# Two residual sums of a software-pipelined encoder chain: VectorE in place of GpSimd

## The chip, the core and the metric

The kernel runs on one core of a Trainium2 chip. The core has five engines with an instruction queue each: PE (TensorE) multiplies and transposes matrices into PSUM, DVE (VectorE), ACT (ScalarE) and POOL (GpSimd) work element by element, SP issues the transfers. Each engine goes through its own queue strictly in order and waits at semaphores for the others. The metric is the device time of one execution in microseconds (us).

## The reference

The input is `x`, four sequences of 1024 tokens with 128 features, all float32. The reference computes two parts after each other, each with a layer norm in front and a residual sum behind:

```python
x = x + encoder(layernorm(x))       # first part: 8 blocks, the one that the change touches
x = x + local_attention_stack(layernorm(x))   # second part: 6 layers of windowed attention and a gated FFN

# one block of the first part (linear attention)
q, k, v = x @ Wq + bq, x @ Wk + bk, x @ Wv + bv
Q, K = elu(q) + 1, elu(k) + 1
KV, Ksum = sum_n(K * v), sum_n(K)
V = Q * KV / (Q * Ksum + 1e-6)
x = layernorm(gelu(V @ Wo + bo) + x) * s1 + b1          # first residual sum
x = layernorm(gelu(gelu(x @ Wf1 + bf1) @ Wf2 + bf2) + x) * s2 + b2   # second residual sum
```

## The kernel before

Data stand with the 128 features on the partitions and tokens along the free dimension. The first part cuts the 4096 tokens into 8 chunks of 512 columns and runs 8 blocks over them: 64 chunk passes, numbered c = 0 to 63. All of it is written out as one software pipeline. Each engine has its own loop `for s in range(-7, CH)` with CH = 64, and in step s it works on chunks of different stages: queries of chunk s+7, keys, values and their exponentials of s+6, the attention's denominator and product of s+4, the first layer norm of s+3, the two FFN matmuls of s+2, the second sum and norm of s+1, and the end of chunk s. The order within a step is written by hand, apart for each engine, and nothing reorders it: the order in the text is the order in the queue.

What an engine does in a step, in its order:

- DVE: `denominator(s+4)` (L998), `invert(s+4, 1)` (L1004, a reciprocal over half a chunk), `query_min(s+6)` (L964), `norm_stats(s+3, 0)` (L1018 to L1026, the statistics of the first norm), `invert(s+4, 0)` (L1004), `key_min(s+6)` (L960), `query_round(s+6)` (L974), `query_up(s+6)` (L980), `attend(s+4)` (L1011), `norm_stats(s+1, 1)` (the same lines, second norm), `keys_up(s+6)` (L969), `key_values(s+6)` (L987, every second chunk with L991). With the first query of a block there is also `biases` (L955).
- POOL: `second_sum(s+1)` (L406), then `rstd_of` and `shift_of` of the first norm (L393, a power on 128x4; L398, a product on 128x4), the same two for the second norm, and `first_sum(s+4)` (L402).
- ACT: `hidden(s+2, 0)` (L786), `second_norm(s)` (L796), `hidden(s+2, 1)`, an activation table load, `query_exp(s+6)` (L763), `unit(s+3, 0)` (L773, scales with what L393 and L398 made), `key_exp(s+6)` (L759), `first_norm(s+3)` (L781), a table load, `hidden` 2 and 3 (L786), `attn_gelu(s+4)` (L767), `unit(s+1, 1)` (L773), `ff_gelu(s+2)` (L791).
- PE: `hidden(c, 0)` for c = s+2 (L551), `second_back(s)` and `first_turn(s+3)` (L492, four 128x128 transposes each), `hidden` 1, `down` 0 (L556), `key` (L497), `hidden` 3, `down` 1, `hidden` 2, `first_back(s+3)` and `second_turn(s+1)` (L492), `query` and `value` (L497), `project(s+4)` (L526), `down` 2 and 3.

The first sum adds the output of `attn_gelu`, g1, to the chunk's columns of X and writes z1, which `first_turn` transposes into PSUM for the statistics. The second sum adds the output of `ff_gelu`, g2, to x1 and writes z2 for `second_turn`. g1, g2, x1, z1 and z2 lie in SBUF with two buffers each. The semaphores `ga` (`attn_gelu`), `g2_r` (`ff_gelu`), `z1_r` and `z2_r` (`z1_ready`, `z2_ready`) carry these steps.

Of the kernel before, what the change touches and what calls it, by code (L numbers as in the profile page):

```python
# [14 lines left out]
ALU = mybir.AluOpType  # L15
# [53 lines left out]
def build(nc, xT, wa1, wa2, wb, wf, rot, mask, outT):  # L69
    with ExitStack() as ctx:  # L70
        def sb(name, shape):
            return ctx.enter_context(nc.sbuf_tensor(name, shape, F32))
# [10 lines left out]
        X = sb("X", [P, NB * SP1])  # L83
# [43 lines left out]
        mk, mq, K_, den, V_, g1, g2, x1, z1, z2, zn1, zn2 = (parts[2 * i:2 * i + 2] for i in range(12))  # L127
# [55 lines left out]
        def seq_col(b, t):  # L183

            return b * SP1 + 1 + t
# [11 lines left out]
        def live(n):  # L197

            return not isinstance(n, int) or 0 <= n < NT
# [14 lines left out]
        def on(c):  # L214

            return 0 <= c < CH

        def of(c):

            return c // NC, c % NC // UT, c % UT  # L220

        def x_at(c):

            _, b, u = of(c)
            return slice(seq_col(b, COL * u), seq_col(b, COL * u) + COL)
# [20 lines left out]
        def done(l, n, each=1):  # L246

            return each * (l * NT + n + 1) + 1
# [29 lines left out]
        def ln_rstd(pool, k, u, v):  # L278
            pool.wait_ge(LN[k]["stat"][u], 3 * v)
            pool.tensor_tensor(rstd[:, u, :], ve[:, u, :], power[:, 0:4], ALU.pow)\  # L280
                .then_inc(LN[k]["rstd"][u], 1)
# [90 lines left out]
        @block.gpsimd  # L372
        def _(pool):
            pool.memset(ident[:, :], 0.0).then_inc(consts, 1)
            pool.memset(power[:, :], -0.5).then_inc(consts, 1)
            pool.wait_ge(consts, 1)
            pool.affine_select(out=ident[:, :], in_=ident[:, :], compare_op=ALU.not_equal, fill=1.0, base=0,
                               pattern=[[-1, P]], channel_multiplier=1).then_inc(consts, 1)
            pool.memset(X[:, :], 0.0).then_inc(consts, 1)
            pool.memset(Y[:, :], 0.0).then_inc(consts, 1)  # L380
            pool.wait_ge(consts, 5)

            def pre_norm(k):
                with pool.Fori(0, NB) as b:
                    for u in U:
                        ln_rstd(pool, "pre", u, k * NB + b + 1)

            pre_norm(0)

            def rstd_of(c, i, stat, ready):  # L390
                k = 2 * i + c % 2
                pool.wait_ge(stat, 3 * c + 3)
                pool.tensor_tensor(rstdA[:, k, :], veA[:, k, :], power[:, 0:4], ALU.pow).then_inc(ready, 1)  # L393

            def shift_of(c, i, rstd_r, ready):
                k = 2 * i + c % 2
                pool.wait_ge(rstd_r, c + 1)
                pool.tensor_tensor(shiftA[:, k, :], mnegA[:, k, :], rstdA[:, k, :], ALU.mult).then_inc(ready, 1)  # L398

            def first_sum(c):  # L400
                pool.wait_ge(ga, c + 1)
                pool.tensor_tensor(z1[c % 2], g1[c % 2], X[:, x_at(c)], ALU.add).then_inc(z1_r, 1)  # L402

            def second_sum(c):
                pool.wait_ge(g2_r, c + 1)
                pool.tensor_tensor(z2[c % 2], g2[c % 2], x1[c % 2], ALU.add).then_inc(z2_r, 1)  # L406

            for s in range(-7, CH):
                if on(s + 1):
                    second_sum(s + 1)  # L410
                if on(s + 3):
                    rstd_of(s + 3, 0, st1_r, rs1_r)
                    shift_of(s + 3, 0, rs1_r, sh1_r)
                if on(s + 1):
                    rstd_of(s + 1, 1, st2_r, rs2_r)
                    shift_of(s + 1, 1, rs2_r, sh2_r)
                if on(s + 4):
                    first_sum(s + 4)
            pre_norm(1)


            for u in U:
                pool.wait_ge(x_done[u], NB * (BLOCKS + 2) + 1)
            pool.memset(PTd, 0.0).then_inc(consts, 1)
            pool.memset(kTf, 0.0).then_inc(consts, 1)
            pool.memset(vv[RING - 1], 0.0).then_inc(consts, 1)
            with pool.Fori(0, LAYERS) as l:
                def add_k(n):
                    pool.wait_ge(rotk_r, done(l, n))
                    pool.wait_ge(trk_mm, done(l, n - 1))  # L430
                    pool.tensor_tensor(tu[:, K], t1[:, K], t2[:, K], ALU.add).then_inc(addk_r, 1)  # L431

                def add_q(n):
                    pool.wait_ge(rotq_r, done(l, n))
                    pool.wait_ge(trq_mm, done(l, n - 1))
                    pool.tensor_tensor(tu[:, Q], t1[:, Q], t2[:, Q], ALU.add).then_inc(addq_r, 1)  # L436

                def probs_norm(n):
                    pool.wait_ge(rec_r, done(l, n))
                    pool.tensor_tensor(pe3, pe3, rr[:, :].unsqueeze(1).unsqueeze(3).to_broadcast([P, 2, HEADS, WIN]),  # L440
                                       ALU.mult).then_inc(p_r, 1)

                def unit_k(n):

                    pool.wait_ge(roots_r, done(l, n, ROOT_STEPS))
                    pool.wait_ge(addk_r, done(l, n))
                    pool.tensor_tensor(heads(tu[:, K]), heads(tu[:, K]), wide(rinv[:, HEADS:2 * HEADS], DH),  # L447
                                       ALU.mult).then_inc(k_r, 1)

                def unit_q(n):  # L450

                    pool.wait_ge(addq_r, done(l, n))
                    pool.tensor_tensor(heads(tu[:, Q]), heads(tu[:, Q]), wide(rinv[:, 0:HEADS], DH),  # L453
                                       ALU.mult).then_inc(q_r, 1)

                def step(n, r):
                    if live(n + 1):
                        add_k(n + 1)
                        add_q(n + 1)
                    if live(n - 1):  # L460
                        probs_norm(n - 1)
                    if live(n + 1):
                        unit_k(n + 1)
                        unit_q(n + 1)

                walk(pool, step)
                with pool.Fori(0, NB) as b:
                    for u in U:
                        ln_rstd(pool, "nf", u, l * NB + b + 1)
# [453 lines left out]
        def _(dve):  # L923
# [38 lines left out]
            def query_min(c):  # L962
                dve.wait_ge(qp_mm, c + 1)
                dve.tensor_scalar(mq[c % 2], ps[:, Q_BANK, :], bias(c, 1), 0.0, ALU.add, ALU.min).then_inc(mq_r, 1)  # L964
# [18 lines left out]
            def key_values(c):  # L983
                _, b, u = of(c)
                dve.wait_ge(vp_mm, c + 1)
                dve.wait_ge(K_r, c + 1)
                dve.scalar_tensor_tensor(K_[c % 2], ps[:, V_BANK, :], bias(c, 2), K_[c % 2], ALU.add, ALU.mult,  # L987
                                         accum_out=kvp[:, b % 2, u, 1:2]).then_inc(KV_r, 1)
                if u == UT - 1:
                    dve.wait_ge(KV_r, c + 1)  # L990
                    dve.tensor_tensor(kvs[:, b, :], kvp[:, b % 2, 0, :], kvp[:, b % 2, 1, :], ALU.add)\  # L991
                        .then_inc(ksum, 1)
# [21 lines left out]
            def norm_stats(c, i, turned, st):  # L1014
# [10 lines left out]
                dve.tensor_scalar(mnegA[:, k, :], mvA[:, k, :, 0], -1.0, None, ALU.mult)  # L1025
                dve.tensor_scalar(veA[:, k, :], mvA[:, k, :, 1], EPS_A, None, ALU.add).then_inc(st, 1)  # L1026

            for s in range(-7, CH):
                if on(s + 4):
                    denominator(s + 4)  # L1030
                    invert(s + 4, 1)
                if on(s + 6):
                    if (s + 6) % NC == 0:
                        biases(s + 6)
                    query_min(s + 6)
                if on(s + 3):
                    norm_stats(s + 3, 0, t1_mm, st1_r)
                if on(s + 4):
                    invert(s + 4, 0)
                if on(s + 6):  # L1040
                    key_min(s + 6)
                    query_round(s + 6)
                    query_up(s + 6)
                if on(s + 4):
                    attend(s + 4)
                if on(s + 1):
                    norm_stats(s + 1, 1, t2_mm, st2_r)
                if on(s + 6):
                    keys_up(s + 6)
                    key_values(s + 6)  # L1050
            for u in U:
                dve.wait_ge(x_done[u], NB * (BLOCKS + 1) + 1)
            pre_norm(1)
# [2 lines left out]
            with dve.Fori(0, LAYERS) as l:  # L1056
# [3 lines left out]
                for i in range(4):  # L1060
                    s = WB[:, B_SC + i * DH:B_SC + (i + 1) * DH].unsqueeze(1).to_broadcast([P, TS, DH])
# [215 lines left out]
```

## Time and profile before

| | before |
|---|---|
| median of 3 runs | 4459.96 us (4459.77 to 4462.57) |
| the profiled execution | 4460.07 us, its span 4458.3 us |
| first part's pipeline | from about 45 us to about 880 us of the span |
| busy over the whole span: PE, DVE, ACT, POOL | 86%, 79%, 76%, 53% |

The span is what the instructions cover; the execution's time is 1.8 us longer. The whole-span shares mix two parts with different limits. The change stands in the first part alone, so only rows of that part's steady stretch, with its fill and its drain, say what an edit there is worth. In the rows below, a busy instruction's start and duration are in us; "idle before" in brackets names the releaser of a wait. Two instructions that follow each other on DVE or ACT overlap by 0.05 to 0.1 us in the records, so the distance between two starts is what an instruction takes of its queue, and durations are a little longer.

### The profile page before, as it was taken

The page shows a single profiled execution, that of the slowest core. Times are in us where ns is not written, and L with a number is a line of the kernel's source. Part 1 is how long each engine was busy: PE and PEld are TensorE (multiplying, and loading weights), DVE is VectorE, ACT ScalarE, POOL GpSimd, SP SyncE. Part 2 cuts the span into 40 slices and gives each one's busy share as a digit, 9 for nine tenths or more (in the row PEclk, how much of TensorE's full clock was granted, in tenths as well). Part 3 has the DMA queues.
Part 4 walks back from the last instruction along what each step waited for, and adds up shares of the span by engine and source line. Part 5 has one row for each costly group of instructions (what it writes and reads, how often), then busy time and mean ns, then how long its engine had stood idle before and what let it go on. Part 6 is the DMA issues. An engine that isn't in the chain of part 4 may idle for free.

```text
span 4458.3 us, 132631 instructions
## 1 busy us (share of the span) xinstructions
PE 3846.2 (86%) x49248; PEld 2440.5 (55%) x49248; DVE 3501.2 (79%) x7236; ACT 3407.2 (76%) x9277; POOL 2377.6 (53%) x1420
## 2 busy tenths in 40 slices
PE   5999999869997699977899877999679997789977
PEld 2444444446664366653566634666436665366653
DVE  6999999679994689954899747999369995589964
ACT  3999999759995489963899836999349995389973
POOL 2444444357772377741777605777137773277750
PEclk8999999989998899988999989999889998899998
DMA  1000000013332033330333302333113332033330
GB/s 45 8 8 10 8 8 26 1 43 81 85 84 55 23 78 83 84 80 7 72 84 82 81 23 56 84 85 81 43 34 81 85 84 65 13 77 84 83 71 19
DMA packets 146282, 245.44 MB, mean 55 GB/s; under 512 B 43664, under 2 KB 69264, under 8 KB 144912
## 3 DMA queue, kind: packets, MB, share of 16 engines
q1 hardware_dynamic: 146064, 242.61, 22.9%
q8 instruction: 127, 2.08, 0.2%
q14 instruction: 91, 0.75, 0.1%
HBM read 26.43 MB, written 2.10 MB: 6 GB/s over the span
## 4 chain that ended last, share of the span: by engine, by line
PE 42%; ACT 27%; SPq 10%; issue 8%; DVE 7%; DMA 3%; POOL 2%; DVEq 0%; ACTq 0%; POOLq 0%
ACT arena L856 12%; PE ps L607 7%; PE ps L722 6%; ACT arena L872 5%; PE ps L556 5%; PE ps L551 5%; ACT arena L831 4%; PE ps L676 4%; PE ps L497 4%; SPq L336 3%; PE ps L731 3%; SPq L346 3%; PE ps L492 3%; DMA arena<-arena 3%; ACT arena L843 2%
## 5 line engine op out<-in xcount | busy, mean ns | idle before, releaser
L607 PE MATMUL ps<-WB,arena 128*128 128x512 f32 x2304 | 1102.3, 615 | 95.0 <-ACT arena L872 37.8
L856 ACT ACTIVATE arena<-arena,nmx 128x64 f32<-128x64 f32 x3072 | 1022.7, 337 | 12.1 <-DVE arena L1145 11.7
L607 PEld LDWEIGHTS ps<-WB,arena 128*128 128x128 f32 x2304 | 418.9, 195 | 510.8 <-issue 451.8
L431 POOL TENSOR_TENSOR arena<-arena 128x1024 f32<-128x1024 f32 x192 | 455.4, 2372 | 400.1 <-DVE arena L1075 397.9
L440 POOL TENSOR_TENSOR arena<-arena,rr 128x1024 f32<-128x1024 f32 x192 | 367.6, 1915 | 466.7 <-DVE rr L1139 466.7
L1068 DVE TENSOR_TENSOR arena<-ps,tables 128x1024 f32<-128x1024 f32 x384 | 468.5, 1220 | 168.9 <-ACT arena L831 168.5
L856 ACT ACTIVATION_READ_ACCUMULATOR arena<-arena,nmx 128x1 f32 x3072 | 585.6, 191 | 0.0
L676 PE MATMUL ps<-arena 128*64 128x64 f32 x12288 | 431.5, 232 | 132.8 <-DMA arena<-arena 108.4
L831 ACT ACTIVATE arena<-ps 128x1024 f32<-128x1024 f32 x384 | 388.5, 1015 | 177.1 <-PE ps L607 142.4
L676 PEld LDWEIGHTS ps<-arena 128*64 128x64 f32 x12288 | 408.6, 146 | 159.6 <-issue 157.4
L1075 DVE TENSOR_TENSOR arena<-ps,tables 128x512 f32<-128x512 f32 x768 | 491.1, 681 | 0.0
L637 PE MATMUL ps<-ident,arena 128*128 128x128 f32 x3072 | 413.9, 279 | 77.3 <-POOL arena L447 40.1
L637 PEld LDWEIGHTS ps<-ident,arena 128*128 128x128 f32 x3072 | 349.9, 143 | 210.6 <-POOL arena L447 99.5
L436 POOL TENSOR_TENSOR arena<-arena 128x1024 f32<-128x1024 f32 x192 | 455.1, 2370 | 7.0 <-PE ps L637 3.6
L1092 DVE TENSOR_REDUCE ssq<-arena 128x32 f32<-128x2048 f32 x192 | 437.0, 2276 | 0.0
L684 PE MATMUL ps<-arena,WB 128*128 128x128 f32 x3072 | 387.1, 281 | 20.1 <-ACT arena L864 20.1
L280 POOL TENSOR_TENSOR rstd<-ve,power 128x4 f32<-128x4 f32 x64 | 63.6, 1009 | 633.7 <-DVE ve L276 633.7
L872 ACT ACTIVATE arena<-ps 64x1024 f32<-64x1024 f32 x384 | 388.7, 1012 | 13.6 <-PE ps L607 11.4
L684 PEld LDWEIGHTS ps<-arena,WB 128*128 128x128 f32 x3072 | 368.4, 196 | 23.0 <-ACT arena L864 23.0
L447 POOL TENSOR_TENSOR arena<-arena,rinv 128x1024 f32<-128x1024 f32 x192 | 365.5, 1903 | 22.1 <-DVE rinv L1123 22.1
L661 PEld LDWEIGHTS ps<-arena 64*32 64x32 f32 x24576 | 267.5, 105 | 190.9 <-issue 185.8
L453 POOL TENSOR_TENSOR arena<-arena,rinv 128x1024 f32<-128x1024 f32 x192 | 365.7, 1905 | 0.0
(101 smaller groups left out, 6751.8 us busy)
## 6 DMA issues: line engine op xcount, KB each, us to landing
arena<-arena SPq DMA_DIRECT2D x768, 128.0 KB, 2.3
arena<-arena SPq DMA_DIRECT2D x1536, 64.0 KB
WB<-wb SPq DMA_DIRECT2D x6, 2176.0 KB, 8.6
arena<-X SPq DMA_DIRECT2D x384, 32.0 KB, 1.8
arena<-wa SPq DMA_DIRECT2D x8, 581.0 KB, 3.7
WF<-wf SPq DMA_DIRECT2D x6, 537.5 KB, 3.8
keep<-xT SPq DMA_DIRECT2D x1, 2048.0 KB, 7.7
outT<-keep SPq DMA_DIRECT2D x1, 2048.0 KB, 6.3
```

The lines of the kernel that those rows point to most:

```text
L431: pool.tensor_tensor(tu[:, K], t1[:, K], t2[:, K], ALU.add).then_inc(addk_r, 1)
L436: pool.tensor_tensor(tu[:, Q], t1[:, Q], t2[:, Q], ALU.add).then_inc(addq_r, 1)
L607: i = pe.matmul(banks[:, c, :], xs_[r], WB[:, w * INNER + c * COL:w * INNER + (c + 1) * COL], start=True, stop=True)
L637: i = pe.transpose(s_ps[:, j // 4, (j % 4) * P:(j % 4 + 1) * P], src[:, j * P:(j + 1) * P], ident[:, :])
L676: i = pe.matmul(o_ps[64 * a:64 * a + 64, side, c * 64:(c + 1) * 64], vv[r][:, side, h * DH:(h + 1) * DH], pw[:, side, :, a, c, :], start=T ...
L684: i = pe.matmul(o_ps[:, 0, 0:P], WB[:, B_WO + c * D:B_WO + (c + 1) * D], OT[:, c, :], start=(c == 0), stop=(c == NP - 1))
L831: act.activation(sq[:, half], src.rearrange("p b c -> p (b c)"), ACT.Square).then_inc(count, 1)
L856: i = act.activation(pe3[:, :, h, :], sc[:, 64 * h:64 * h + 64].rearrange("p (k q) -> p k q", k=2), ACT.Exp, bias=nmx[:, h:h + 1], accum_o ...
L872: i = act.activation(vv[r][rows, side, :], kv_ps[rows].rearrange("p b c -> p (b c)"), ACT.Copy)
L1068: dve.tensor_tensor(heads(t1[:, half]), src.rearrange("p b (h d) -> p (b h) d", d=DH), t, ALU.mult)
L1075: k = dve.tensor_tensor(heads(t2[:, half])[:, :, here], src.rearrange("p b (h d) -> p (b h) d", d=DH)[:, :, there], t, ALU.mult)
L1092: dve.tensor_reduce(ssq[:, :], heads(sq), AX_X, ALU.add).then_inc(red_r, 1)
```

## The change

The two functions `first_sum` and `second_sum` leave the POOL loop and stand in the DVE loop, with the same operands, the same waits and the same signals. `second_sum(s+1)` comes behind `query_min(s+6)` and ahead of `norm_stats(s+3, 0)`; `first_sum(s+4)` is the last thing of DVE's step. POOL keeps the powers and products on 128x4. No other engine's program changes.

```diff
@@ gpsimd
-            def first_sum(c):
-                pool.wait_ge(ga, c + 1)
-                pool.tensor_tensor(z1[c % 2], g1[c % 2], X[:, x_at(c)], ALU.add).then_inc(z1_r, 1)
-
-            def second_sum(c):
-                pool.wait_ge(g2_r, c + 1)
-                pool.tensor_tensor(z2[c % 2], g2[c % 2], x1[c % 2], ALU.add).then_inc(z2_r, 1)
-
             for s in range(-7, CH):
-                if on(s + 1):
-                    second_sum(s + 1)
                 if on(s + 3):
                     rstd_of(s + 3, 0, st1_r, rs1_r)
                     shift_of(s + 3, 0, rs1_r, sh1_r)
                 if on(s + 1):
                     rstd_of(s + 1, 1, st2_r, rs2_r)
                     shift_of(s + 1, 1, rs2_r, sh2_r)
-                if on(s + 4):
-                    first_sum(s + 4)
@@ vector
+            def first_sum(c):
+                dve.wait_ge(ga, c + 1)
+                dve.tensor_tensor(z1[c % 2], g1[c % 2], X[:, x_at(c)], ALU.add).then_inc(z1_r, 1)
+
+            def second_sum(c):
+                dve.wait_ge(g2_r, c + 1)
+                dve.tensor_tensor(z2[c % 2], g2[c % 2], x1[c % 2], ALU.add).then_inc(z2_r, 1)
+
             for s in range(-7, CH):
                 if on(s + 4):
                     denominator(s + 4)
...
                     query_min(s + 6)
+                if on(s + 1):
+                    second_sum(s + 1)
                 if on(s + 3):
                     norm_stats(s + 3, 0, t1_mm, st1_r)
...
                     key_values(s + 6)
+                if on(s + 4):
+                    first_sum(s + 4)
```

DVE's queue before, one step of the steady stretch from its last instruction on; the names in brackets are the semaphores that an instruction waits for:

```order
601 L987 SCALAR_TENSOR_TENSOR arena,kvp<-ps,arena 128x512 [waits K_ready,v_proj]
602 L991 TENSOR_TENSOR kvs<-kvp 128x2 [waits KV_ready]
603 L998 TENSOR_SCALAR arena<-arena,kvs 128x512 [waits seq_sums]
604 L1004 RECIPROCAL arena<-arena 128x256 [waits den_ready]
605 L964 TENSOR_SCALAR arena<-ps,arena 128x512 [waits q_proj]
606 L1018 BN_STATS statA<-ps 128x6 [waits z1_turned]
```

The same place of DVE's queue in the changed kernel (its lines are numbered 12 lower up to the two new functions):

```order
600 L975 SCALAR_TENSOR_TENSOR arena,kvp<-ps,arena 128x512 [waits K_ready,v_proj]
601 L979 TENSOR_TENSOR kvs<-kvp 128x2 [waits KV_ready]
602 L1018 TENSOR_TENSOR arena<-arena,X 128x512 [waits attn_gelu]
603 L986 TENSOR_SCALAR arena<-arena,kvs 128x512 [waits seq_sums]
604 L992 RECIPROCAL arena<-arena 128x256 [waits den_ready]
605 L952 TENSOR_SCALAR arena<-ps,arena 128x512 [waits q_proj]
606 L1022 TENSOR_TENSOR arena<-arena 128x512 [waits ff_gelu]
607 L1006 BN_STATS statA<-ps 128x6 [waits z1_turned]
```

The first sum (602) with its wait for `attn_gelu` now stands ahead of the denominator, the reciprocal and the query minimum, and the second sum (606) with its wait for `ff_gelu` ahead of the first norm's statistics. POOL's queue before, one step:

```order
103 L402 TENSOR_TENSOR arena<-arena,X 128x512 [waits attn_gelu]
104 L406 TENSOR_TENSOR arena<-arena 128x512 [waits ff_gelu]
105 L393 TENSOR_TENSOR rstdA<-veA,power 128x4 [waits n1_stats]
106 L398 TENSOR_TENSOR shiftA<-mnegA,rstdA 128x4 [waits n1_rstd]
107 L393 TENSOR_TENSOR rstdA<-veA,power 128x4 [waits n2_stats]
108 L398 TENSOR_TENSOR shiftA<-mnegA,rstdA 128x4 [waits n2_rstd]
```

Afterwards only the four instructions on 128x4 are left of it.

## Rows read from the trace of the kernel before

**Rows 1.** Busy time by engine in stretches of the first part (start:end, length, then engines)
```profile
core 0: us, PE busy (x) PEld busy (x) DVE busy (x) ACT busy (x) POOL busy (x), PEclk, DMA share, GB/s
100.00:820.00 720.00, 719.71 (x2353) 353.76 (x2352) 661.38 (x1912) 684.79 (x1175) 290.23 (x352) 1.00 0.03 11
...
844.00:856.00 12.00, 10.34 (x34) 4.84 (x34) 3.63 (x24) 8.80 (x19) 4.74 (x6) 1.00 0.01 1
```

**Rows 2.** Waits from 100 to 900 us (total us, times, longest): DVE, PE
```profile
DVE statA L1018 <- PE ps L492: 66.4, 97, 8.7
...
PE ps L492 <- POOL arena L406: 1.3, 1, 1.3
```

**Rows 3.** PE in order of time: back transposes of two steps in a row, and a late one
```profile
501.27 1.08 PE L492 MATMUL ps<-ident,arena 128*128 128x128 f32 x8
...
513.50 1.08 PE L492 MATMUL ps<-ident,arena 128*128 128x128 f32 x8
...
819.20 1.08 PE L492 MATMUL ps<-ident,arena 128*128 128x128 f32 x8
```

**Rows 4.** ACT in order of time, the same step
```profile
501.96 0.78 ACT L781 ACTIVATE arena<-ps,arena 128x512 f32<-128x512 f32 x1 [0.23 <-PE ps L492]
502.75 1.28 ACT L786 ACT_TABLE_LOAD   x1
504.05 1.27 ACT L786 ACTIVATE arena<-ps,arena 128x512 f32<-128x512 f32 x2
505.20 0.69 ACT L767 ACTIVATE arena<-ps,arena 128x512 f32<-128x512 f32 x1
...
507.15 0.73 ACT L791 ACTIVATE arena<-ps,arena 128x512 f32<-128x512 f32 x1
...
511.94 1.49 ACT L773 ACTIVATE arena<-ps,shiftA,rstdA 128x128 f32<-128x128 f32 x4
```

**Rows 5.** DVE in order of time, the same step
```profile
502.39 0.89 DVE L1018 BATCH_NORM_STATS2 statA<-ps 128x6 f32<-128x128 f32 x4 [0.49 <-PE ps L492]
...
505.73 0.49 DVE L998 TENSOR_SCALAR arena<-arena,kvs 128x512 f32<-128x512 f32 x1
506.25 1.75 DVE L1004 RECIPROCAL arena<-arena 128x256 f32<-128x256 f32 x1
507.92 0.65 DVE L964 TENSOR_SCALAR arena<-ps,arena 128x512 f32<-128x512 f32 x1
508.55 0.89 DVE L1018 BATCH_NORM_STATS2 statA<-ps 128x6 f32<-128x128 f32 x4
...
511.69 0.65 DVE L960 TENSOR_SCALAR arena<-ps,arena 128x512 f32<-128x512 f32 x1
512.26 0.42 DVE L974 TENSOR_SCALAR arena<-arena 128x512 f32<-128x512 f32 x1
...
513.38 0.74 DVE L1011 SCALAR_TENSOR_TENSOR arena<-arena,kvs 128x512 f32<-128x512 f32 x1
```

**Rows 6.** POOL in order of time, the same step and the next
```profile
505.97 1.38 POOL L402 TENSOR_TENSOR arena<-arena,X 128x512 f32<-128x512 f32 x1 [0.63 <-ACT arena L767]
507.95 1.28 POOL L406 TENSOR_TENSOR arena<-arena 128x512 f32<-128x512 f32 x1 [0.60 <-ACT arena L791]
...
518.21 1.10 POOL L402 TENSOR_TENSOR arena<-arena,X 128x512 f32<-128x512 f32 x1 [0.63 <-ACT arena L767]
```

**Rows 7.** All engines in the drain: a first norm's statistics and the scaling that waits for them
```profile
826.48 0.89 DVE L1018 BATCH_NORM_STATS2 statA<-ps 128x6 f32<-128x128 f32 x4 [0.54 <-PE ps L492]
...
829.47 1.51 ACT L773 ACTIVATE arena<-ps,shiftA,rstdA 128x128 f32<-128x128 f32 x4 [1.44 <-POOL shiftA L398]
```

**Rows 8.** A DVE sum of two SBUF operands; a DVE start released by ACT
```profile
879.95 1.30 DVE L935 TENSOR_TENSOR arena<-keep,X 128x512 f32 x2 [5.44 <-ACT X L796]
...
1409.75 0.69 ACT L917 ACTIVATE arena<-ps,WF 128x512 f32<-128x512 f32 x1
1410.58 0.75 DVE L1192 SCALAR_TENSOR_TENSOR arena<-ps,WF,arena 128x512 f32<-128x512 f32 x1 [5.12 <-ACT arena L917]
```

## The prediction, made before the changed kernel was run

> **What bounds the kernel now.** I read the first part alone: first the busy time by engine in its steady stretch, then the waits, then each engine in order of time over one step.
>
> The busy times [rows 1] show three engines close to full: from 100 to 820 us PE is busy for 719.71 of 720 us, ACT for 684.79, DVE for 661.38, and POOL, which carries the two sums, for 290.23. The granted clock there is 1.00, TensorE's upper level of 2.4 GHz.
>
> The length of a step comes from PE's back transposes (`first_back` and `second_turn`, L492) [rows 3]: they start at 501.27, at 513.50, and 26 steps later at 819.20, so a step takes (819.20 - 501.27) / 26 = 12.23 us. In 720 us there are 58.9 steps. DVE is thus busy for 661.38 / 58.9 = 11.23 us of a step and idle for 1.00 us, nearly all of it while it waits for transposes (66.4 us in 97 waits) [rows 2].
>
> What closes the step of 12.23 us is a loop between ACT and PE, not DVE and not POOL. I call the start of `first_back` F (501.27) and follow it. ACT's `first_norm` starts at F + 0.69, its table load at F + 1.48, `hidden` 2 and 3 at F + 2.78, `attn_gelu` at F + 3.93 and ends at F + 4.62 [rows 4]. From there ACT runs on, with two short waits for PE, to `unit(s+3)` at 511.94, and 1.56 us later PE starts the next `first_back` at 513.50 [rows 3, 4]. The statistics of DVE and the power of POOL come in time for that `unit`: the statistics start at 508.55 [rows 5]; in the drain, where ACT does wait for them, the distance from the statistics' start to `unit` is 829.47 - 826.48 = 2.99 us [rows 7]; so `unit` could start at 511.54 and starts at 511.94. That is a slack of 0.40 us. It is the number on which the forecast turns.
>
> The sums themselves are off this loop before the change. POOL's first sum starts 0.08 us behind `attn_gelu`, its second 0.07 us behind `ff_gelu` [rows 4, 6], and from 100 to 900 us PE waits once, for 1.3 us, for the second [rows 2].
>
> **What goes.** Two POOL instructions a step, 1.10 to 1.38 and 1.28 us [rows 6], 64 of each. Their readers, two groups of transposes, hardly ever wait for them, so I take a gain of 0. Its bounds are 0 and, if the 1.3 us of wait [rows 2] were all of it, about 1 us in the whole run. The exception is the very end, where nothing else is left to hide the last second sum: it gets some 0.5 us shorter, which I leave out.
>
> **What comes.** Two DVE sums of 128x512 float32 from SBUF. The trace of before has the same operation on DVE in L935, two in 1.30 us [rows 8], that is 0.61 us from start to start and 0.69 us for the last. The bounds for one in the queue are 0.57 us (a 128x512 form with one tensor operand, 511.69 to 512.26 [rows 5]) and 0.69 us. I take 0.61, since it is the same operation. DVE's own work becomes 11.23 + 1.22 = 12.45 us, already over the 12.23 us of a step.
>
> A rule speaks for the move: the Trainium skill, page "GPSIMD Engine Reference", section "4.1 Engine selection", sends elementwise sums to VectorE because GpSimd takes about twice as long. The trace agrees on the ratio (1.28 against 0.69 us, 1.9 times); what it would make of the time is the second rival below.
>
> **What moves, and where it gets on the path.** The changed order puts a wait for `attn_gelu` ahead of everything that DVE does in the next step. `attn_gelu` ends at F + 4.62 (505.89), and DVE before the change starts `denominator` already at 505.73, F + 4.46 [rows 4, 5]. So DVE now stands at the first sum until `attn_gelu` is through. Queued behind it are `denominator`, half of the reciprocals, `query_min`, the second sum and then the first norm's statistics, for which POOL, ACT and PE wait. The new chain, once round:
>
> - F to the end of `attn_gelu`: 4.62 us [rows 4].
> - ACT's end to DVE's start: 1410.58 - (1409.75 + 0.69) = 0.14 us [rows 8]; bounds 0.08 us (POOL's start behind ACT [rows 4, 6]) and some 0.2. I take 0.13.
> - first sum 0.61, `denominator` 0.52 (505.73 to 506.25), reciprocal 1.67 (to 507.92), `query_min` 0.57 (511.69 to 512.26, the same form without a wait behind it), second sum 0.61 [rows 5, 8]: 3.98 us.
> - statistics to `unit`: 2.99 us [rows 7].
> - `unit` to the next F: 1.56 us [rows 3, 4].
>
> The sum is 4.62 + 0.13 + 3.98 + 2.99 + 1.56 = 13.28 us against 12.23: **1.05 us more in each step**. The same seen from the slack: the statistics start 8.73 us behind F instead of 7.28 (508.55 - 501.27), 1.45 us later, of which 0.40 is slack.
>
> What else could be later is not. The second sum needs `ff_gelu`, which ends at F + 6.61 (507.15 + 0.73); DVE gets to it at F + 8.12. `first_turn` needs z1; the first sum ends at F + 5.4, and the transposes run one `second_back` behind `unit(s+1)`, after F + 6.2. The second norm's statistics start at F + 1.12 (502.39) for PE; DVE reaches them at F + 0.9, so they stay where they are, and DVE is ready for the first sum at F + 4.46 at the latest. DVE keeps about 0.2 us of wait there and 0.3 to 0.6 us in front of the first sum. PE gets about 1 us of idle time in front of each `first_back`. ACT waits before `unit`.
>
> **The clock.** The added holes in PE's work could cost granted clock. In the drain PE is busy for 10.34 of 12 us, with holes of that size, at a granted clock of 1.00 [rows 1]; the forecast has it busy for about 12.2 of 13.3 us. I take 0 for it; its bound above is in the last rival.
>
> **The sum.** The chain runs through the first sum and the next step's `query_min` in 61 steps (s = -4 to 56). 61 x 1.05 = 64 us. In the fill and at the last steps single terms differ by some tenths either way, which I leave out. The second part's instructions are the same. The profiled execution of before took 4460.07 us, 0.11 us from the median of the runs: 4460 + 64 = **4524 us**. With the bounds of the terms (each sum 0.57 to 0.69 twice, the start behind ACT 0.08 to 0.2) a step takes 13.15 to 13.51 us, and the time is 4516 to 4538 us.
>
> **The rivals.**
>
> 1. *DVE's own work is the bound, the chain isn't.* If DVE need not stand at `attn_gelu` (because ACT drifts ahead of it once DVE is slower), a step takes DVE's work alone: 12.45 us by its busy time, or 12.65 with the small gaps between its instructions, 0.22 to 0.42 us more, 61 steps: 4473 to 4486 us. For it: ACT has 12.23 - 684.79 / 58.9 = 0.60 us of idle time. Against it: `attn_gelu` hangs at a fixed distance behind F by ACT's own order, a table load and three activations, and F hangs on DVE's statistics. Chance 0.10.
> 2. *Faster: the slow sum was what PE waited for.* If POOL's second sum stood between `ff_gelu` and the transposes on the path, each step would win 1.28 - 0.69 = 0.59 us, 61 x 0.59 = 36 us: 4424 us. It decides where the second sum ends later than PE gets to `second_turn`. That it does not is in the rows: it ends at 509.23, and `second_turn` follows `first_back` of 513.50. The rule of the Trainium skill on elementwise sums ("GPSIMD Engine Reference", section 4.1) points this way. Chance 0.03.
> 3. *No change within what can be told* (0.2%, 9 us; about what a measurement of this kernel tells from no change). DVE's 1.00 us of idle takes the 1.22 us in, and the 0.40 us of slack the rest. It would need the wait for `attn_gelu` to cost nothing, at most 0.15 us a step. Chance 0.03.
> 4. *More than forecast.* Two prices. First, POOL and DVE hinder each other: POOL's first sum took 1.38 us where it started at 505.97, inside L998 (505.73 to 506.22), and 1.10 us in the next step [rows 5, 6]. If a DVE sum met a POOL power like that, 0.28 us a step would come in, 17 us: 4541 us. But the second norm's power and product are over some 3 us behind the statistics of F + 1.12, by F + 4.1, and the first sum starts at F + 4.75. Second, a lower clock at the holes: PE's own work of 12 us at half the clock in one step of ten would cost about 1.2 us a step, 73 us more, some 4597 us. Together 0.08.
>
> The Trainium skill, page "SBUF — State Buffer", section "SBUF: two separate sides", has a rule for the first of these: a DVE operation with two SBUF inputs and a GpSimd operation hold one port pair in turn, the loser waits for the whole instruction. The trace agrees in that L402's long case ends 1.13 us behind the end of L998, its own length. By that rule the move is safe only as long as the two do not meet, and would else cost up to 17 us by the sum above.
>
> **How the numbers follow.** The forecast has 0.76, the rivals 0.10, 0.03, 0.03 and 0.08. 8 in 10 are reached with the forecast's own bounds, 4516 to 4538, widened on both sides for the fill, for terms that I left out and for the milder half of rival 4: 4500 to 4545 us. Rival 1 stays below. Faster by over 0.2%: 0.03; within: 0.03; slower: 0.94.
>
> **What would show it.** Right: in the steady stretch F to F is 13.2 to 13.5 us; the first sum waits for `attn_gelu` L767 in nearly each step, and the statistics no longer wait for PE in front of the first norm; `unit` L773 waits for POOL's L398 about 1 us in each step; PE idles about 1 us in front of L492. Rival 1: no wait at the first sum, DVE over 99% busy. Rival 2: a step under 12.2 us. Wrong altogether: a granted clock below 1.00 from 100 to 820 us, POOL powers longer than 1.0 us, or DVE sums far from 0.69 us.

## The result and the profile after

| | before | after |
|---|---|---|
| median of the runs | 4459.86 us (4457.67 to 4462.57, 4 runs) | 4515.72 us (4514.69 to 4517.39, 4 runs) |
| ratio | | 1.0125, 95% interval 1.0108 to 1.0143 |
| span of the profiled execution | 4458.3 us | 4515.6 us |
| first DVE row of the second part (tables, L1062) | 919.35 us | 979.3 us |

The changed kernel is 56 us slower, by the profiled executions 57. The last line splits it: the second part starts 60 us later and then takes 2.7 us less. The lines of the functions in front of the DVE loop moved up by 12, so L773 of before is L761 here, L767 is L755, L492 is L480, L1018 is L1006.

Busy time of the steady stretch, the same view and columns as [rows 1]:

```profile
100.00:820.00 720.00, 675.99 (x2178) 327.52 (x2178) 677.10 (x1882) 641.64 (x1091) 130.36 (x216) 1.00 0.03 10
```

PE is no longer full (675.99 of 720 us), the granted clock stays at 1.00, its upper level. DVE is busy for 677.10 us and POOL for only 130.36. Now the engines over one step, which answer to [rows 3 to 6]; first PE and ACT:

```profile
510.15 1.09 PE L480 MATMUL ps<-ident,arena 128*128 128x128 f32 x8 [0.77 <-ACT arena L761]
...
523.32 1.09 PE L480 MATMUL ps<-ident,arena 128*128 128x128 f32 x8 [0.77 <-ACT arena L761]
...
510.84 0.78 ACT L769 ACTIVATE arena<-ps,arena 128x512 f32<-128x512 f32 x1 [0.23 <-PE ps L480]
...
514.09 0.69 ACT L755 ACTIVATE arena<-ps,arena 128x512 f32<-128x512 f32 x1
...
521.75 1.51 ACT L761 ACTIVATE arena<-ps,shiftA,rstdA 128x128 f32<-128x128 f32 x4 [0.82 <-POOL shiftA L398]
```

From one `first_back` to the next there are 523.32 - 510.15 = 13.17 us. PE waits for `unit` (L761) in front of it and `unit` waits 0.82 us for POOL's L398. DVE and POOL between them:

```profile
514.82 0.69 DVE L1018 TENSOR_TENSOR arena<-arena,X 128x512 f32<-128x512 f32 x1 [0.24 <-ACT arena L755]
515.42 0.48 DVE L986 TENSOR_SCALAR arena<-arena,kvs 128x512 f32<-128x512 f32 x1
515.94 1.75 DVE L992 RECIPROCAL arena<-arena 128x256 f32<-128x256 f32 x1
517.61 0.65 DVE L952 TENSOR_SCALAR arena<-ps,arena 128x512 f32<-128x512 f32 x1
518.18 0.68 DVE L1022 TENSOR_TENSOR arena<-arena 128x512 f32<-128x512 f32 x1
518.78 0.89 DVE L1006 BATCH_NORM_STATS2 statA<-ps 128x6 f32<-128x128 f32 x4
...
520.43 1.01 POOL L393 TENSOR_TENSOR rstdA<-veA,power 128x4 f32<-128x4 f32 x1 [6.21 <-DVE veA L1014]
...
DVE arena L1018 <- ACT arena L755: 22.5, 62, 1.4
```

The first sum (L1018) waits for `attn_gelu` (L755), 62 times from 100 to 950 us, and behind it come the denominator, the reciprocal, the query minimum, the second sum (L1022) and the statistics, with no gap. This is the chain that was forecast: 510.15 to the end of `attn_gelu` at 514.78, 4.63 us; 0.04 us to the first sum; 3.96 us to the statistics at 518.78; 2.97 us to `unit` at 521.75; 1.57 us to the next `first_back`. Together 13.17.

### The profile page after: what moved, and what is told of

Same layout as the page of the kernel before. It is cut to its first block, busy times and chain, and to the rows that moved or that the text cites. A ratio compares the mean times of both kernels' runs of the same rounds, so it can differ in the third digit from the quotient of the medians.

```text
span 4515.6 us, 132631 instructions
## 1 busy us (share of the span) xinstructions
PE 3861.4 (86%) x49248; PEld 2442.1 (54%) x49248; DVE 3577.0 (79%) x7364; ACT 3414.2 (76%) x9277; POOL 2215.2 (49%) x1292
## 4 chain that ended last, share of the span: by engine, by line
ACT 33%; PE 26%; DVE 15%; SPq 10%; issue 8%; POOL 4%; DMA 3%; DVEq 0%; ACTq 0%; POOLq 0%
ACT arena L844 12%; PE ps L595 7%; PE ps L710 6%; ACT arena L860 5%; ACT arena L819 4%; PE ps L664 4%; SPq L336 3%; PE ps L719 3%; SPq L346 3%; DVE arena L992 2%; DMA arena<-arena 2%; ACT arena L831 2%; ACT arena L836 2%; SPq L337 2%; ACT arena L761 2%
## 5 line engine op out<-in xcount | busy, mean ns | idle before, releaser
L393 POOL TENSOR_TENSOR rstdA<-veA,power 128x4 f32<-128x4 f32 x128 | 128.9, 1007 | 726.1 <-DVE veA L1014 726.1
L860 ACT ACTIVATE arena<-ps 64x1024 f32<-64x1024 f32 x384 | 388.6, 1012 | 13.3 <-PE ps L595 11.0
L435 POOL TENSOR_TENSOR arena<-arena,rinv 128x1024 f32<-128x1024 f32 x192 | 365.1, 1902 | 21.3 <-DVE rinv L1123 21.3
```

The costliest lines, as they stand in the source:

```text
L860: i = act.activation(vv[r][rows, side, :], kv_ps[rows].rearrange("p b c -> p (b c)"), ACT.Copy)
```

## The experiments

Every kernel computes all that the reference asks for. The times of one kernel scatter by 3 to 19 us. Much of that lies in the second part: the profiled executions of before and e11, whose second parts start within 0.1 us of each other, have spans of 4458.3 and 4450.5 us. So two numbers of each profiled execution stand beside the medians: the step of the first part, and the start of the second part (first row of the tables on DVE) against the 919.35 us of before. The start holds some scatter too: the first `first_norm` of all starts between 84.64 and 88.47 us, by kernel, so a difference of 1 or 2 us in that column tells nothing. Where two steps are given they take turns; every eighth step, with `biases`, is 0.1 us longer in most kernels with a sum on DVE. Each ratio is against executions of the kernel before that were run beside that kernel (medians 4459.07 to 4460.11 us), and so are the differences named below. The last column is explained with the last three kernels.

| kernel | step, us | second part starts | median, us | ratio (95%) | DVE idle at layer starts |
|---|---|---|---|---|---|
| before | 12.23 | 919.35 | 4459.86 | | 13.5 us |
| after | 13.17 | +60.0 | 4515.72 | 1.0125 (1.0108 to 1.0143) | 13.5 |
| e1_second_only | 12.23 / 12.37 | +3.1 | 4453.09 | 0.9986 (0.9976 to 0.9995) | 1.1 |
| e2_first_only | 12.56 | +27.8 | 4475.11 | 1.0031 (1.0019 to 1.0042) | 1.1 |
| e3_first_behind_den | 12.64 / 12.84 | +30.3 | 4491.1 | 1.0072 (1.0056 to 1.0089) | 13.6 |
| e4_second_behind_stats | 12.93 | +44.3 | 4503.98 | 1.0104 (1.0085 to 1.0122) | 13.6 |
| e5_second_behind_recip | 12.63 / 12.70 | +28.2 | 4489.46 | 1.0066 (1.0049 to 1.0082) | 13.5 |
| e6_pad_in_wait | 13.17 | +60.0 | 4508.8 | 1.0109 (1.0092 to 1.0126) | 1.1 |
| e7_pad_in_chain | 13.30 | +67.5 | 4517.37 | 1.0139 (1.0122 to 1.0156) | 1.1 |
| e8_both_moved | 12.42 / 12.63 | +21.0 | 4479.15 | 1.0044 (1.0028 to 1.0061) | 13.3 |
| e9_before_64 | 12.23 | -1.5 | 4447.38 | 0.9974 (0.9963 to 0.9986) | 1.1 |
| e10_e1_64 | 12.23 / 12.37 | +4.3 | 4462.61 | 1.0003 (0.9994 to 1.0012) | 13.7 |
| e11_before_32 | 12.23 | -0.1 | 4459.17 | 0.9998 (0.9988 to 1.0008) | 13.3 |

### One sum alone

e1_second_only, against the changed kernel (e2_first_only does the same with the other sum):

```diff
@@ gpsimd
+                if on(s + 4):
+                    first_sum(s + 4)          # on pool, as before
@@ vector
-                if on(s + 4):
-                    first_sum(s + 4)
```

> Second sum on DVE behind the query minimum, first sum left on POOL. Chain theory: DVE no longer stands at attn_gelu; it leaves the second norm's statistics (F + 1.13) 3.02 us or, every other step, 3.34 us later, then denominator 0.51, reciprocal 1.67, query_min 0.57, sum 0.60, statistics to unit 2.97, unit to F 1.57. That is 12.04 and 12.36 us, of which the first is under the 12.23 us that the loop of ACT and PE takes anyway: 12.30 us on average, 61 steps of 0.07: about 4464 us, hardly to be told from before. If the price were that of DVE's work as such (half of the 56 us for each sum), 4488 us.

> First sum on DVE as the last of its step, second sum left on POOL. Chain theory: F to F is the 13.17 us of the changed kernel less one sum of 0.60 us: 12.57 us, 0.34 more than before, 61 steps: 4481 us, with a wait for attn_gelu in front of the first sum in each step. DVE-work theory A (a sum costs only where DVE's total work of 11.84 us goes over the step of 12.23 us): 4460 us. Theory B (half of the loss for each sum): 4488 us.

Of e1, ACT's `first_norm` in two steps, and then of e2, two steps in a row:

```profile
504.10 0.78 ACT L775 ACTIVATE arena<-ps,arena 128x512 f32<-128x512 f32 x1 [0.23 <-PE ps L486]
...
516.47 0.78 ACT L775 ACTIVATE arena<-ps,arena 128x512 f32<-128x512 f32 x1 [0.23 <-PE ps L486]
```
```profile
505.97 1.09 PE L486 MATMUL ps<-ident,arena 128*128 128x128 f32 x8 [0.17 <-ACT arena L767]
...
518.54 1.09 PE L486 MATMUL ps<-ident,arena 128*128 128x128 f32 x8 [0.16 <-ACT arena L767]
```

The steps are what the chain gives: 12.37 us in every other step of e1 (64 sums of 0.60 us, 38 us more of DVE work, put the start of the second part off by 3 us, and the time from the first `first_norm` to the last grows by 5), 12.57 in e2. The two sums cost very unequal amounts: with half of the loss for each, both kernels would have their second part 30 us later. e2 has it 27.8 us later, near that by itself; e1, with 3.1 us, is the one that rules the halves out. It is the first sum's place, a wait for ACT in front of DVE's next step, that costs. With it in place the second sum costs its whole 0.60 us (13.17 against 12.57); without it, next to nothing.

Two things were not as expected. The medians are below what the steps say: e1 is 7 us faster than before, although its second part starts 3 us later, and e2 is 15 us slower, where its second part starts 28 us later; that is taken up below. And in e2 every eighth step takes 13.08 us. DVE and POOL in such a step:

```profile
147.01 0.52 DVE L949 TENSOR_SCALAR bias<-arena 128x2 f32<-128x2 f32 x1
147.45 0.74 DVE L958 TENSOR_SCALAR arena<-ps,arena 128x512 f32<-128x512 f32 x1
...
146.24 1.27 POOL L402 TENSOR_TENSOR arena<-arena 128x512 f32<-128x512 f32 x1 [2.61 <-ACT arena L785]
```

L949 (`biases`, L955 of before) works on 128x2 and takes 0.10 us elsewhere. Here it meets POOL's second sum, which started at 146.24, and ends at 147.53, with POOL's end at 147.51. L949 has a median of 0.52 us over its eight executions in e2. The rows read as a POOL operation that holds up a small DVE operation until it is through. This is the direction of the port that the prediction had not looked for.

### The order within DVE's step

e3_first_behind_den and e5_second_behind_recip, each against the changed kernel; e8_both_moved does both, e4_second_behind_stats puts the second sum directly behind `norm_stats(s + 3, 0)`:

```diff
@@ e3, vector
                     denominator(s + 4)
+                if on(s + 3):
+                    first_sum(s + 3)
...
-                if on(s + 4):
-                    first_sum(s + 4)
@@ e5, vector
-                if on(s + 1):
-                    second_sum(s + 1)
...
                     invert(s + 4, 0)
+                if on(s + 1):
+                    second_sum(s + 1)
```

> Both sums on DVE, the first one place further down: behind the denominator of the next step, the second as in the changed kernel. DVE then never stands at attn_gelu. Chain theory: the wait of 0.24 to 0.43 us in front of the first sum goes, and the chain runs through DVE alone from the second norm's statistics on: F + 1.13 + 3.02 or 3.34 + 0.51 + 0.60 + 1.67 + 0.57 + 0.60 + 2.97 + 1.57 = 12.64 or 12.96 us, 12.80 on average, 61 steps of 0.57: 4495 us. If DVE's order did not matter, only its work: 4516 us as the changed kernel.

> First sum as in the changed kernel, second sum on DVE directly behind the first norm's statistics, where POOL's power (L393) starts. If DVE and POOL do not hinder each other: the second sum is off the chain, 12.57 us by that chain, but DVE gets to the second norm's statistics 0.4 us later, 12.57 and 12.79 us by turns, 12.68 on average: 4487 us, POOL's power stays at 1.01 us. If a DVE sum of two SBUF operands keeps the power from starting until it is through (it would start 2.16 instead of 1.65 us behind the statistics, or last that much longer): 13.09 us a step, 4512 us.

> First sum as in the changed kernel, second sum on DVE behind the second half of the reciprocals (invert(s+4, 0)), when POOL's power and product of the first norm are through. Chain theory: 12.57 us by the chain through attn_gelu, 12.79 us in every other step by DVE's own work: 12.68 on average: 4487 us. POOL's power 1.01 us. If the place of the second sum did not matter: 4516 us.

> Both sums on DVE, the first behind the next step's denominator, the second behind the second half of the reciprocals. Chain theory: no chain through attn_gelu or through the second sum is left, and DVE's own work is the bound, 12.46 and 12.78 us by turns, 12.62 on average, 0.39 more than before: 4484 us, DVE over 99% busy. It shows the floor of any order that keeps both sums on DVE. If more than DVE's work is at play, it stays clearly above.

With the same 128 sums on DVE the loss goes from 56 us to 31 (e3), 30 (e5) and 20 (e8). DVE's work is the same in all four, so the work as such accounts for 20 of the 56 us at most, and the place of the sums for the rest. The steps of e3 (12.64 and 12.84 us, where 12.64 and 12.96 were expected) and of e5 (12.63 and 12.70 for 12.57 and 12.79) are close to the chains, not exactly on them. e8 leaves next to no wait in DVE's step:

```profile
core 0: us, PE busy (x) PEld busy (x) DVE busy (x) ACT busy (x) POOL busy (x), PEclk, DMA share, GB/s
100.00:820.00 720.00, 711.93 (x2289) 351.36 (x2289) 699.90 (x1980) 679.13 (x1144) 137.38 (x228) 1.00 0.03 10
```

DVE's records cover 97% of the stretch, where over 99% was expected; the gaps are those between its own instructions, and it waits for others twice, 1.8 us in all. The step is 12.52 us on average, 0.10 less than the distances that I had added up. Since DVE hardly waits any more, this is about the floor of the move: with both sums on DVE and none of them on the chain it is still 20 us slower than before.

e4 is the test of the port between DVE and POOL. POOL's power and the DVE sum in front of it, in e4:

```profile
510.57 0.68 DVE L1022 TENSOR_TENSOR arena<-arena 128x512 f32<-128x512 f32 x1
...
510.75 1.38 POOL L393 TENSOR_TENSOR rstdA<-veA,power 128x4 f32<-128x4 f32 x1 [5.54 <-DVE veA L1014]
512.20 0.20 POOL L398 TENSOR_TENSOR shiftA<-mnegA,rstdA 128x4 f32<-128x4 f32 x1
...
516.84 1.01 POOL L393 TENSOR_TENSOR rstdA<-veA,power 128x4 f32<-128x4 f32 x1 [4.44 <-DVE veA L1014]
```

The power that meets the sum takes 1.38 us, the other of the same step, which meets none, 1.01. The 0.37 us are on the chain: 12.57 + 0.37 = 12.94, measured 12.93. So e4 lies between its two expectations: the power does not start later, it lasts longer, and by less than the 0.51 us that I had put down. e5, with the sum 1.7 us later in DVE's step, gets them back.

### A small instruction in two places

e6_pad_in_wait puts a copy of 128x128 in front of `first_sum(s + 4)`, e7_pad_in_chain the same copy in front of `second_sum(s + 1)`:

```diff
+                if on(s + 4):
+                    dve.tensor_copy(pad[:, :], rotary[:, 0, 0:2, :].rearrange("p a b -> p (a b)"))
```

> The changed kernel with one more DVE instruction in each step, a copy of 128x128 from SBUF to SBUF (some 0.15 to 0.2 us of the queue), in front of the first sum. Chain theory: DVE waits there for attn_gelu 0.24 to 0.43 us anyway, so it costs 0: 4516 us. DVE-work theory: 62 times 0.17, 4526 us.

> The same extra copy of 128x128, but behind the query minimum, in front of the second sum. Chain theory: it lies between the first sum and the statistics and costs its whole length in each step, 62 times 0.17: 4526 us. If DVE's idle time in front of the first sum could take it: 4516 us.

The two kernels hold the same instructions. DVE around the copy, of e6 and then of e7:

```profile
501.21 0.22 DVE L1051 COPY pad<-rotary 128x128 f32<-128x128 f32 x1
501.73 0.69 DVE L1019 TENSOR_TENSOR arena<-arena,X 128x512 f32<-128x512 f32 x1 [0.29 <-ACT arena L756]
```
```profile
508.36 0.22 DVE L1034 COPY pad<-rotary 128x128 f32<-128x128 f32 x1
508.50 0.69 DVE L1023 TENSOR_TENSOR arena<-arena 128x512 f32<-128x512 f32 x1
```

In e6 it goes into the wait: the step stays at 13.17 us and the second part starts at the same +60.0 us. In e7 it takes 0.14 us of the queue, the step is 13.30 us, the second part starts at +67.5. The whole times are 8.6 us apart. The idle time in front of the first sum is usable, and only for what stands there. This rests on the steps and the starts, and on the two kernels side by side: e7's median alone, 4517.37 us, is what was expected if the idle time could take the copy. Both medians have a surplus over the starts, as in e1 and e2: e6 is 49.7 us slower than before with a start 60.0 later, e7 58.3 with 67.5. That is 10 and 9 us, and 10 and 13 in e1 and e2; in the changed kernel it is 4.

### Where the surplus comes from

Among DVE's waits in the second part one line tells the kernels apart. Before:

```profile
DVE tables L1062 <- issue: 13.5, 5, 2.9
```

and in e6, e7 and e2 in its place, here of e7:

```profile
DVE tables L1065 <- DVE X L1202: 1.1, 5, 0.2
```

At the start of layers 2 to 6 of the second part DVE stands still for 2.7 us each in front of the tables, with nothing that the profile shows as its cause ("issue"). Counted in DVE's queue ahead of the layer loop, the kernels in which it does hold 0 or 128 instructions more than before (before, after, e3, e4, e5, e8), those in which it does not 64 or 192 more (e1, e2, e6, e7). The count is of instructions that compute; a moved sum also brings its wait for a semaphore, a copy does not. Three kernels test the number by itself, with copies of 128x4 placed where DVE waits for the second norm's transposes: e9_before_64 is the kernel before with 64 of them, e10_e1_64 is e1 with 64, e11_before_32 is before with 32 (every other step).

```diff
+                if on(s + 1):
+                    dve.tensor_copy(pad[:, :], rotary[:, 0, 0, 0:4])
                 if on(s + 1):
                     norm_stats(s + 1, 1, t2_mm, st2_r)
```

> The kernel before, both sums on POOL, with 64 more DVE instructions in the first part: a copy of 128x4, placed where DVE waits for the second norm's transposes 0.49 us. In the runs so far DVE stood idle about 2.7 us in front of L1062 at the start of layers 2 to 6 of the second part (13.3 to 13.6 us in sum, released by 'issue') in the kernels whose DVE queue holds 0 or 128 instructions more than before, and not in those with 64 or 190 to 192 more. If it is the number of DVE instructions ahead of the layer loop that does it, not the sums: first part as before (12.23 us a step), that idle time gone, 8 to 12 us less: 4448 to 4452 us. If the number does not matter: 4460 us.

> The kernel with the second sum alone on DVE, with the same 64 small DVE copies more. By the number of DVE instructions (128 more than before): the idle time in front of L1062 of layers 2 to 6 returns, 13.5 us in sum, and the time is the first part's 3 us over before: 4462 us or a little more. If the number does not matter: 4453 us as without the copies.

> The kernel before with 32 small DVE copies more, in every other step. By the number of DVE instructions it is between the two known cases and tells where the idle time in front of L1062 begins: either 13.5 us in sum and 4460 us, or about 1 us in sum and 4448 to 4452 us, or something between. No theory prefers one.

The DVE waits of e9, e10 and e11, one line of each in this order:

```profile
DVE tables L1065 <- DVE X L1202: 1.1, 5, 0.2
```
```profile
DVE tables L1065 <- issue: 13.7, 5, 2.9
```
```profile
DVE tables L1065 <- issue: 13.3, 5, 2.9
```

With 64 instructions that compute nothing the kernel before gets 12 us faster, at the same granted clock of 0.943 over the span of both profiled executions; e1 with 64 more loses its gain. The small tile that the copies write is not the cause, since e10 and e11 have it and stand still. So the gain of e1 over before (7 us) does not come from the moved sum: its first part is 3 us longer, and its second part lost a standstill that depends on how many DVE instructions stand ahead of the loop. The start of the second layer in before and in e9:

```profile
1505.96 2.50 DVE L1062 TENSOR_TENSOR tables<-rotary,WB 128x512 f32<-128x512 f32 x4 [2.67 <-issue]
```
```profile
1502.58 2.50 DVE L1065 TENSOR_TENSOR tables<-rotary,WB 128x512 f32<-128x512 f32 x4 [0.21 <-DVE X L1202]
```

That it has to do with where the loop's instructions lie, and with fetching them at the jump back, is argued and not shown; the runs show the dependence on the count (0, 32 and 128 more: there; 64 and 192 more: not there), not the mechanism. e9, at 4447.38 us, is the fastest kernel of this study, ahead of before (ratio 0.9974, 0.9963 to 0.9986) and of the changed one.

## Why the prediction was right

The forecast was 4524 us with 4500 to 4545; measured are 4515.72. The chain that was named is the one that the profile shows, so the number is not right by luck alone. But 4515.72 lies just below the 4516 to 4538 us that the bounds of the terms gave, and two things that were left out, some 3 us more at the start of the pipeline and 4 us less in the second part, nearly cancel. Point by point:

- **The chain.** The loop through `attn_gelu`, the first sum, DVE's next step up to the statistics, POOL, `unit` and `first_back` is the bound; each of its waits is in the profile, and e6 and e7 show that an instruction costs on it and costs nothing beside it. Forecast 13.28 us a step, measured 13.17. The terms: to the end of `attn_gelu` 4.62 against 4.63; sums and what stands between 3.98 against 3.96; statistics to `unit` 2.99 against 2.97; `unit` to `first_back` 1.56 against 1.57. The term that was mis-sized is ACT's end to DVE's start: 0.13 put down, from one row of the second part, 0.04 measured. It was even below the bound of 0.08 that I had taken from POOL. Over all steps from 100 to 900 us it is 0.03 or 0.04. It accounts for 0.09 of the 0.11 us.
- **The sum.** 61 steps of 1.05 us were 64 us. 61 of 0.94 are 57, which is also what lies between the second `first_norm` and the last (57.4 us more than before), and the second part starts 60 us later. Of the 3 us between, 2 are the fill, which I had left out (the distance of the first two `first_norm` is 14.06 us, where it was 12.08); the first `first_norm` itself starts 1.4 us later, which is within the scatter of that start, and behind the last `first_norm` 0.8 us are saved. The whole time grew by 56 and not by 60: the second part was 2.7 us shorter in the profiled execution. Both kernels have the same standstill at the layers' starts (13.5 us), so that is not the reason; it is within the scatter of the second part.
- **The slack of 0.40 us** in front of `unit` held: the statistics start 8.63 us behind `first_back` (518.78 - 510.15) instead of 7.28 [rows 3, 5], 1.35 later, of which 0.94 arrive in the step.
- **Rival 1** (DVE's work alone) gave 4473 to 4486 us. It is wrong for this order, since DVE waits at the first sum in every step; it is right for e8, 4479.15 us, where both sums are taken off the chain.
- **Rival 2** (faster): neither sum on POOL was on the path. e1 moves the second sum alone and its first part gets 3 us longer. Its whole time is lower than before by 7 us, and would have been taken for this rival without the count of instructions.
- **Rival 3** (no change) needed the wait for `attn_gelu` to cost at most 0.15 us a step; 0.94 arrived in each.
- **Rival 4** (DVE and POOL hinder each other) did not decide here: POOL's L393 stays at 1.01 us in the changed kernel, since the first sum (514.82) starts 0.6 us behind the end of POOL's last product (514.22), as worked out (0.65). Its price was real: 0.37 us a step in e4, where 0.28 had been put down. The Trainium skill, page "SBUF — State Buffer", section "SBUF: two separate sides", says that of a GpSimd operation and a DVE operation with two SBUF inputs, or in a 2-port perf mode, whichever starts first keeps the port pair for its whole instruction. The rows agree in direction (POOL's power behind a DVE sum in e4, DVE's small operation behind POOL's sum in e2), though in e4 the record of the loser starts in time and is 0.37 us longer, not the whole overlap of 0.50. L949 in e2, like L998 in the prediction, has one tensor input; whether it ran in such a mode no row shows.
- **The clock** stayed at 1.00, with PE busy for 94% of the stretch; it was 1.00 too in the drain of before, with PE busy for 10.34 of 12 us [rows 1].
- **The signs.** `unit` waits 0.82 us for POOL and PE 0.77 us for `unit`, both somewhat less than the 1 us named, and the statistics no longer wait for PE in the steady stretch.

## What to carry to other kernels

In a pipeline written out by hand, follow the loop that closes a step and write down the slack at each place where another engine joins it: here 0.40 us of slack stood against a delay of 1.35 us, and DVE's busy time alone (92% before) gave only the 13 to 26 us of rival 1, which fit e8 and not the changed kernel. A wait put at the end of an in-order queue's step is a wait in front of the whole next step; with the same sum one place further down (e3) the kernel took 25 us less. And when a small change of one part moves the whole time by a few tenths of a per cent, look at where the parts start before giving the change the credit.

## What was not expected of the hardware

- DVE stood still for 2.7 us at each of five starts of a loop body, 13.5 us in sum, depending on the number of DVE instructions ahead of the loop: there with 0, 32 and 128 more than before, gone (0.2 us each) with 64 and 192 more. 64 small copies in a wait made the kernel 12 us faster. The mechanism is not shown.
- A DVE instruction that waits for ACT (L1018, two SBUF inputs) started 0.03 or 0.04 us behind ACT's end in every step from 100 to 900 us. In the row of the second part that the prediction used (L1192, which also reads PSUM) it was 0.14 us, though DVE had been standing there too, for 5.12 us. Why the two differ is open.
- A DVE operation on 128x2 that started under a POOL sum of two SBUF operands took 0.52 instead of 0.10 us; a DVE sum made a POOL power on 128x4 0.37 us longer (1.38 instead of 1.01 us).
